# Input, gate and summed state weights in float16 parts instead of float32 ones, chunk 0 in unsplit float32 products, and a new order of the loop

## The reference, cut to what matters

```python
# for each token, with q = layernorm(x) and k = v = ctx (16 heads)
r = decay * r + k * v                       # elementwise carry
inp = (q * r) @ Wi.T + bi
gate = sigmoid(inp @ Wg.T + bg)
blended = gate * state + (1 - gate) * inp
state = tanh(blended @ A.T + inp @ Bm.T)    # the next token needs this one
out = state @ Wo.T + bo
# afterwards, for all tokens
x1 = x + tanh(g_xattn) * out
h = relu(layernorm(x1) @ ternary(W1).T + b1)        # width 1024
y = x1 + tanh(g_ffn) * (h @ ternary(W2).T + b2)
# ternary(W) = clip(round(W / (mean|W| + 1e-5)), -1, 1)
```

## Time and profile before

| | |
|---|---|
| three runs | 311.37, 310.77, 311.32 us; median 311.32 |
| the profiled execution, whole | 311.31 us |
| its span, first to last instruction | 309.5 us |
| start, up to the first tanh of chunk 0 | 0 to 19.92 us |
| turns 0, 1 and 2 | up to about 70 us |
| one turn of `body` | 16.75 us |
| busy in the span | PE 95%, DVE 87%, ACT 81%, POOL 42% |
| mean granted TensorE clock | 0.994 of full speed |

### The profile page before, as it was taken

The page is one execution under the profiler, slowest core; times in us unless marked ns, Lnnn a source line. Parts: engine busy times, 40 slices in busy tenths (PEclk is TensorE's granted clock), DMA queues, the critical chain, the costliest instruction groups (busy, mean ns, idle before and its releaser), DMA issues.

```text
span 309.5 us, 9519 instructions
## 1 busy us (share of the span) xinstructions
PE 295.2 (95%) x3595; PEld 261.2 (84%) x3595; DVE 267.9 (87%) x872; ACT 252.1 (81%) x604; POOL 128.6 (42%) x276
## 2 busy tenths in 40 slices
PE   6999899999999999999999999999999999986995
PEld 4777777897989899898989898989989898965784
DVE  5777999999999999999999999999999999686563
ACT  3677787978889898988888888899898887766593
POOL 3664025172634435262727263453526271613220
PEclk9999999999999999999999999999999999999899
DMA  7954214316264644546362626464464426271221
GB/s 261 390 159 111 68 37 105 67 19 123 101 105 137 102 140 70 169 72 167 54 151 64 123 100 104 136 103 140 71 172 71 103 40 129 43 133 21 51 36 68
DMA packets 21726, 33.39 MB, mean 108 GB/s; under 512 B 2096, under 2 KB 10544, under 8 KB 21552
## 3 DMA queue, kind: packets, MB, share of 16 engines
q0 software_dynamic: 10736, 12.06, 26.0%
q1 hardware_dynamic: 10512, 20.19, 19.1%
q10 hardware_dynamic: 432, 0.53, 0.6%
HBM read 16.52 MB, written 4.19 MB: 67 GB/s over the span
## 4 chain that ended last, share of the span: by engine, by line
PE 77%; DVE 13%; ACT 3%; issue 3%; POOL 2%; DMA 1%; DVEq 0%; POOLq 0%; ACTq 0%
PE y_ps L1401 16%; PE hid_ps L1388 15%; PE inp_ps L1309 9%; PE pre_ps L1340 7%; PE pre_ps L1260 6%; PE att_ps L1361 6%; PE pre_ps L1346 5%; PE ret_ps L1282 4%; PE ret_ps L1272 2%; PE ret_ps L1291 2%; PE att_ps L1370 2%; DVE w_q L1050 1%; DVE mix L894 1%; DVE m_hi L900 1%; DVE h_lo L956 1%
## 5 line engine op out<-in xcount | busy, mean ns | idle before, releaser
L585 ACT ACTIVATE state<-pre_ps,tanh_unit 128x64 f32<-128x64 f32 x120 | 37.0, 309 | 24.8 <-PE pre_ps L1346 24.4
L1401 PE MATMUL y_ps<-w_q,h_hi 128*128 128x256 bf16 x240 | 57.2, 275 | 0.0
L1401 PE MATMUL y_ps<-w_q,h_lo 128*128 128x256 bf16 x240 | 57.1, 275 | 0.0
L1388 PE MATMUL hid_ps<-xt_lo,w_q 128*128 128x256 f16 x240 | 55.5, 272 | 0.0
L1388 PE MATMUL hid_ps<-xt_hi,w_q 128*128 128x256 f16 x240 | 55.5, 272 | 0.0
L560 ACT ACTIVATE hid<-hid_ps,b_s 128x256 f32<-128x256 f32 x120 | 49.9, 471 | 0.6 <-PE hid_ps L1388 0.6
L1340 PE MATMUL pre_ps<-m_hi,a_hi 128*128 128x32 f16 x508 | 42.3, 178 | 5.3 <-DVE m_hi L900 4.4
L1340 PEld LDWEIGHTS pre_ps<-m_hi,a_hi 128*128 128x128 f16 x508 | 35.7, 96 | 11.1 <-DVE m_hi L900 7.2
L894 DVE SCALAR_TENSOR_TENSOR mix<-state,unit,inp 128x64 f32<-128x64 f32 x120 | 33.3, 278 | 9.8 <-ACT state L585 6.6
L1340 PE MATMUL pre_ps<-m_hi,a_lo 128*128 128x32 f16 x508 | 41.5, 176 | 0.0
L956 DVE TENSOR_TENSOR h_lo<-hid,h_hi 128x512 f16<-128x512 f32 x60 | 39.8, 683 | 0.6 <-ACT h_hi L566 0.4
(11 more groups left out here) (219 smaller groups left out, 851.7 us busy)
## 6 DMA issues: line engine op xcount, KB each, us to landing
x_norm<-x_rows_in SPq DMA_DIRECT2D x16, 256.0 KB, 2.8
cx<-ctx_in SPq DMA_DIRECT2D x16, 256.0 KB, 3.2
x_res<-x_in SPq DMA_DIRECT2D x16, 256.0 KB, 3.5
x_res<-bo_g POOLq DMA_DIRECT2D x16, 256.0 KB, 5.0
x<-b_g POOLq DMA_DIRECT2D x15, 256.0 KB, 3.9
y_out<-y SPq DMA_DIRECT2D x15, 256.0 KB, 2.0
y<-x POOLq DMA_DIRECT2D x13, 256.0 KB, 3.3
w_raw<-w_in SPq DMA_DIRECT2D x2, 512.0 KB, 7.2
```

What stands on the lines that cost most here:

```text
L585: nc.scalar.activation(state[:, q[1] % 2, :, step_cols(j)], pre_ps[q[1] % 2][:, :].rearrange("p (k n) -> p k n", k=K)[:, :, step_cols(j)], ...
L1388: last = nc.tensor.matmul(hid_ps[p % 2][:, u * N:(u + 1) * N], w1_q[:, k, cut], v[:, par, k, :], start=n == 0, stop=n == len(terms) - 1)
L1401: last = nc.tensor.matmul(y_ps[:, t * D:(t + 1) * D], h[:, f, t * P:(t + 1) * P], w2_q[:, f, :], start=f == 0 and t == 0 and h is h_hi, st ...
```

## The change

The gate weights and A + Bm get float16 parts, scaled by a power of two from their maximum; `inp` gets float16 parts too. Chunk 0 now has a bound and a unit as the others have, and its two products, with the gate weights and with A + Bm, are unsplit float32 (`first_gate`, `first_from_inp`); `from_rest`, the float32r parts of Bm and A and what made them are gone. Step 0 of chunk 0 becomes a real step. A + Bm is added on POOL in SBUF, not by a second load and an adding DMA. Half of the ternary weights (W2) are made by ACT alone, with a rounding and a sign. The order of `body`, `first`, `second` and `third` is new on PE, ACT, DVE and POOL.

```diff
-        wg_hi, wg_lo = sb("wg_hi", [P, K, D], f32r), sb("wg_lo", [P, K, D], f32r)
+        wg_hi, wg_lo = sb("wg_hi", [P, K, D], f16), sb("wg_lo", [P, K, D], f16)
-        c_hi, c_lo = sb("c_hi", [P, K, D], f32r), sb("c_lo", [P, K, D], f32r)
+        c_hi, c_lo = sb("c_hi", [P, K, D], f16), sb("c_lo", [P, K, D], f16)
-        inp_hi, inp_lo = sb("inp_hi", [P, K, N], f32r), sb("inp_lo", [P, K, N], f32r)
+        inp_hi, inp_lo = sb("inp_hi", [P, K, N], f16), sb("inp_lo", [P, K, N], f16)
...  SP
-            for n in (WG, WA, BM):
+            for n in (WA, BM, WG):
-            sp.dma_start(c_sum[:, :, :], wsq_in[BM]).then_inc(bm_again, 16)
...  POOL, start: the sum of the weights, after growth, bound_of and scales_of of chunk 0
+            nc.gpsimd.tensor_tensor(c_sum[:, :, :], wsq[WA][:, :, :], wsq[BM][:, :, :], ALU.add).then_inc(c_added, 1)
-            pool.dma_start(c_sum[:, :, :], wsq[WA][:, :, :], accum_op=ALU.add).then_inc(c_added, 16)
...  POOL, body: the new order
+                if norm:
+                    rstd1_of(norm)
+                    bound_of(norm)
                 if project:
                     scales_of(project)
+                if chain and peeled != NC - 1:
+                    add_bo(chain)
                 if exists(plus(c, -3)):
                     add_x1(plus(c, -3))
                 if attend:
                     rstd2_of(attend)
                     shift2_of(attend)
+                    add_b2(attend)
                 if norm:
                     shift1_of(norm)
...  PE: the two unsplit products of chunk 0
+            def first_gate(k):
+                pe.wait_ge(inp_set, K if k else 1)
+                for m in range(K):
+                    last = nc.tensor.matmul(FIRST_GATE[m][:, m * N:(m + 1) * N], wsq[WG][:, k, m * P:(m + 1) * P],
+                                            inp[:, 0, k, :], start=k == 0, stop=k == K - 1)
+            def first_from_inp(k):
+                pe.wait_ge(act_prep, adone["c_whole"])
+                for m in range(K):
+                    nc.tensor.matmul(pre_ps[0][:, m * N:(m + 1) * N], c_whole[:, k, m * P:(m + 1) * P], inp[:, 0, k, :],
+                                     start=k == 0 and m == 0, stop=False, skip_group_check=True)
...  ACT: a quarter of W2 in two operations
+            def whole(n):
+                nc.scalar.activation(round_of(n), quarter((w1_raw, w2_raw)[w], piece), ACT.Identity,
+                                     bias=whole_up[:, :], scale=per_mean[:, w:w + 1]).then_inc(rounded, 1)
+            def whole_sign(n):
+                nc.scalar.activation(quarter((w1_q, w2_q)[w], piece), round_of(n), ACT.Sign,
+                                     bias=whole_down[:, :]).then_inc(act_prep, 1)
```

More of the change, by code:

```diff
@@ L719, in body @@
                 peeled = c[1]
+                if norm:
+                    carry(project)
+                    square(norm)
                 if attend:
                     state_high(attend)
-                if exists(plus(c, -3)):
-                    y_out(plus(c, -3))
                 if project:
@@ L746, in body @@
                 if project:
+                    inp_out(project, 1)
                     inp_high(project)
@@ L754, in body @@
                     end_state_high(0)
-                if norm:
-                    carry(project)
+                if attend:
+                    x1_apply(attend)
+                if ffn:
+                    hidden_high(ffn, 2)
+                if chain:
+                    tanh_step(chain, 5)
                 if ffn:
@@ L759, in body @@
                     hidden_high(ffn, 3)
-                if attend:
-                    x1_apply(attend)
-                if chain:
-                    tanh_step(chain, 5)
-                if norm:
-                    norm_apply(norm)
+                if project:
+                    gate_out(project)
                 if chain:
@@ new lines, in gated_state @@
+                nc.vector.scalar_tensor_tensor(out=mix[:, :, :], in0=before, scalar=unit[:, par:par + 1],
+                                               in1=inp[:, par, :, step_cols(j)], op0=ALU.mult,
+                                               op1=ALU.subtract).then_inc(mix_set, 1)
+                if j == 0:
+                    dve.wait_ge(gate_set, upto(q))
+                dve.wait_ge(mix_set, upto(q, T, j + 1))
+                nc.vector.tensor_tensor(m_hi[:, :, :], mix[:, :, :], now, ALU.mult).then_inc(m_hi_set, 1)
@@ L1080, in second @@
                 gated_state(NEXT_CHUNK, 0)
+                norm_stats(FOURTH)
                 state_low(CHUNK)
-                scaled_low("wo", wo_hi, wo_lo, WO, S_WO)
                 gated_state(NEXT_CHUNK, 1)
                 unit_of(THIRD)
+                norm_mean(FOURTH)
+                retain(THIRD)
                 ternary(0)
@@ L1130, in third @@
                 normed_low(NEXT_CHUNK)
-                scan(FIFTH)
             def body(c):
@@ L1571, in body @@
                 if ffn:
-                    y_product(ffn, 2)
-                if project:
-                    from_inp(project, 0)
-                    from_inp(project, 1)
-                if ffn:
-                    y_product(ffn, 3)
-                if chain:
-                    step(chain, 5)
+                    y_product(ffn, 0)
                 if project:
```

613 lines of the change are left out of this document (298 added, 315 removed).

## The result

The changed kernel takes 314.06 us (median of 14 runs), the kernel before 311.36 (14 runs) on the same chip: ratio 1.0089, 95% interval 1.0064 to 1.0113. It is 0.9% slower; I had forecast 304.8. One of the changed kernel's 14 runs took 357.84 us, at a mean granted clock of 0.75, and the ratio leaves it out. The profiled execution is 313.85 whole, span 312.0, against 311.31 and 309.5.

The account below looks back on a forecast made before the run. PE was taken to bound the turns until DVE ends last. From 311.31 us, 1.5 up to turn 3, 3.2 in the turns less 0.2, and 2.0 at the end make 6.5: 304.8 us, range 303 to 306.5.

Parts of the forecast that it names:

- the sentence on SP: Loads behind the store: store moves about 4.5 us later, yet x and cx land two or more microseconds before use.
- POOL far late: Rival: x1_t waits behind rstd2, add_bo holds POOL 2.2 us; turns of 17.35, 315.2 us; chance 0.10.
- The bound of the turn: Loop turns: PE can be shortened by half a microsecond, until DVE's list without waits, about 16.1 us, ends last.
- The widths: from_inp and gate products in float16 take 1.31 us each, saving 0.12 and 0.20, together 0.32 a turn.
- the width is worth nothing: Rival: float16 runs at float32r's pace, the order alone leaves 16.7 a turn, 307.8 us; chance 0.05.
- POOL: Loop turns: moved rstd1 takes 0.76, add_bo 1.13, so POOL reaches rstd2 some 0.7 us before x1_mean is there.
- both POOL rivals: rstd2 late on POOL: turns of 16.9, 309.8 us, chance 0.14; or turns of 17.35, 315.2 us, chance 0.10.
- my gain of "nearly 1.0" in turn 1: Turn 1: gains nearly 1.0 us from four ternary operations fewer on DVE and no normed_t ahead of turn 2.
- Turn 0: Turn 0: gives back about 0.35 us, as c_hi, wg_hi and wo_hi stand ahead of tanh 3 on ACT.
- The start: Up to the first tanh: 18.6 instead of 19.92 us, a gain of 1.3, bounds 0.3 and 1.8.
- The last turn: Last turn: longest PE pause about 1.7 instead of 2.3 us, so the clock holds: 1.9 us, bounds 0 and 2.5.

Follow-up runs that it names:

- e1: Changed kernel with x_norm and cx loaded on SP one turn further ahead and ahead of the store; 310.03 us, ratio to the kernel before 0.9949.
- e3: Changed kernel with add_x1 ahead of add_bo on POOL; 310.51 us, ratio to the kernel before 0.9963.
- e4: Kernel before, old order of work, with the parts of input, gate weight, summed state weights and chunk 0's weights and rest as float16; 310.95 us, ratio 0.9973.
- e12: e11 with POOL's bound_of moved behind shift2_of; 307.62 us, ratio to the kernel before 0.9883.
- e9: e6 with PE's four transposes of normed_t, ahead of step 1, issued twice in turns 4 to 14; 313.0 us, ratio to the kernel before 1.0046.
- e5: e1 with the parts of input, gate weight and summed state weights back as float32r; 310.55 us, ratio to the kernel before 0.9965.
- e8: e6 with PE's four transposes of x1_t, behind step 5, issued twice in turns 3 to 15; 311.27 us, ratio to the kernel before 0.9965.
- e6: e1 with shift1_of(FOURTH) ahead of add_b2 on POOL and ACT's whole(4), (5), (6) moved into turn 1; 307.77 us, ratio to the kernel before 0.9879.
- e2: Changed kernel with square back behind tanh 1 and y_out on ACT, and bound_of behind add_x1 on POOL; 313.35 us, ratio 1.0057.
- e7: e6 with keep_warm(46) for keep_warm(34) at the start; 308.34 us, ratio to the kernel before 0.9887.
- e11: e7 with norm_apply behind tanh 7 and state_high, carry and square behind tanh 2, POOL's bound_of behind scales_of; 345.42 us, ratio to the kernel before 1.1073.

## Why the prediction was wrong

**The step that failed for the sign** is the sentence on SP: the loads "follow the store of chunk c-3, which waits for add_x1. That moves about 4.5 us later in the turn, but x and cx are loaded a turn ahead, and land two or more microseconds before" they are used. I had seen the store move and `square` move ahead, and left a margin of 2 us or more between them. The store moved by 5.3 to 6.8 us, from 4.4 behind the first tanh to 9.7 to 11.2; add_x1, now right behind add_bo, lands in 4.7 us instead of 3.3, and cx in 4.3 instead of 3.2 (medians). From the issue of cx's load to the place of `square` in a quiet turn 3.3 to 4.7 us are left, which is what the load takes: the margin is nothing. In five turns of twelve ACT waited, 5.9 us together; e1 gives back 4.6 us of span in the loop, e3 the same. No rival of mine had this place. That my "POOL far late" stands at 315.2, near the 314.06 measured, is chance: its chain is not in this trace.

The "two megabytes less or more" of the same paragraph are a slip: the changed kernel reads 16.26 MB from HBM instead of 16.52.

**The bound of the turn.** I wrote that a microsecond saved on PE is worth one, "until DVE ends last", and put DVE's list without waits at 16.1. The first part failed: 0.32 us less on PE was worth 0.00 in e4. The second is too low by my estimate. In the turn of the earlier trace rows DVE works for 15.62 us, and its idle 1.13 is cut into 24 gaps, of which three are over 0.1 (0.11, 0.11 and 0.18). If the 0.18 and one 0.11 are waits and the others belong to the list, it is some 16.5. A quiet turn after has 15.46 of work and 1.17 of gaps, four of them 0.10 to 0.15, and the shortest turn that any run repeats is 16.57, in e12. That DVE's list holds the turn near there is argued: no run lengthened that list alone, and e9 shows that PE ahead of step 1 has no slack either.

PE's busy time is no evidence: the lengthened turn of 18.16 above, in which the whole loop waited for a transfer, has PE "busy" for 18.10, and e5's and e1's turns differ by 0.16 in the chain's from_inp and gate (1.40 and 1.39 against 1.32 and 1.31) and by 0.01 in length. The Trainium skill says so (Trainium Kernel Development and Optimization, section Performance Expectations): matmul busy time is a bad metric for how close a kernel is to roofline, while MFU, the arithmetic done against the peak, and the busy share of the weight loads are good ones. The trace agrees on the matmuls. The weight loads, 14.6 to 15.4 us in turns where PE is busy throughout, show more, but not the wait alone: they are 16.09 in the lengthened turn and 14.91 in the quiet one, for the same work. Had I weighed the 15.28 in the earlier trace rows, DVE's 15.62 would have been the longest.

**The widths** shrank the products as forecast (from_inp 0.66 a half, the gate 1.31) and were worth 0.00 in the old order (e4) and 0.01 in the new (e5). My rival "the width is worth nothing" had the right result for a wrong reason: the products are faster, but a turn doesn't wait for them. In the new order they lie near the place where e8 found PE with a quarter of a microsecond of slack. The new order is worth 0.10 a turn: 16.75 to 16.65.

**POOL** did what I forecast in the turns (rstd1 0.71, no lateness), so both POOL rivals fell for the loop. The moved rstd1 never ran beside an h_lo, so whether h_lo stretches it was not tried. h_lo does stretch small work: POOL's `bounds`, 0.19 to 0.20 in the loop before, takes 0.65 to 0.66 beside one in turns 3 to 13 after and ends 0.06 behind it.

```profile
196.94 0.68 DVE L963 TENSOR_TENSOR h_lo<-hid,h_hi 128x512 f16<-128x512 f32 x1
197.02 0.65 POOL L343 TENSOR_TENSOR bounds<-old_part,new_part 128x2 f32<-128x2 f32 x1
```

In turn 1, which I laid out in a sentence, the same mechanism cost 1.63: shift1_of behind add_b2. e6 gives 2.0 back there; my gain of "nearly 1.0" in turn 1 would have been 1.7 with its moves. Turn 0 lost 1.37 where I had 0.35. In e1's trace DVE's list is full from tanh 1 to the end of that turn (its idle before a mix is at most 0.3); that this is the cause is argued, not tried.

**The start** gave 0.7 instead of 1.3 at a full clock in both. A part of it may be a_lo, which waits 1.45 for a_hi on ACT; no run moved it.

**The last turn** came out as forecast: no stretch at a lower clock where the earlier trace rows have 0.65, and 2.0 us less. But that is luck. My step was that a longest pause of 1.7 us instead of 2.3 keeps the clock. e4_before_f16_parts, with the old order and a longest pause of PE of 2.21, held its clock there and took 36.0 from turn 15's first tanh on. All twelve profiles with the new order have the same longest pause, 1.45, and differ: the changed kernel's and those of e1, e2, e3 and e5 held the clock, and in the seven others it was 0.5 for 3.4 us of that stretch; e6 and e7 took 37.0. At the same clock the new order is worth 0.5 (37.5 against 37.0, 36.0 against 35.5), the fall costs 1.5 where I had 1.9, and what decides whether it comes stays open.

The sum: 9.0 us of error, of which 4.6 are the load of cx (204.26 less 12 x 16.64), 1.8 the quiet turns, 2.0 turns 0 to 2, and 0.6 the start.

## What to carry to other kernels

When a consumer moves to the head of a turn, follow its load back through the whole queue that issues it, with every wait in front, and price each transfer at what it takes beside the others; a margin of two microseconds is no margin for four links of DMA. Count an engine's list with its gaps before calling another the bound, and test a bound by doubling a small piece of work at two places: where it costs in full there is no slack. A wait put ahead of unrelated work in an in-order queue costs that work, not the waiter.

## What I had not expected of the hardware

- The granted clock at the start differs between executions of one order of work: 1.0 with the first tanh at 18.98 to 19.46 (seven profiles of the new start), or 0.5 for some 3 to 10 us with 20.45 to 22.83 (five). It moves the first tanh by up to 3.6 us (22.83 in e3, 19.24 in the changed kernel), more than the whole effect of the change.
- One line of POOL (bound_of ahead of rstd2_of, with a wait of 2.1 us) made turns of 20.3 out of 16.6. Some 2.3 us are the wait; the other 1.4 are the granted clock, which fell to 0.5 for 3.4 us behind PE's pause in nine turns of eleven. The same pause in turns 3 and 11 left the clock at 1.0.
- A POOL operation on 128x2 elements can last as long as the DVE operation beside it: `bounds` 0.65 us beside h_lo instead of 0.19, and in e11 `shift` 1.26 beside the scan.
